# V' of all 128 tokens by whole-array products, its 32-token windows regrouped by DMA

## What is computed

```
qkv = x @ Wqkv;  q, k, v: 16 heads of 64
q = rotary(l2norm(q) * qs);  k = rotary(l2norm(k) * ks)
# windows of 32 queries against their own 32 keys and the 32 before
sim = q_window @ k_pair^T * 8, masked;  attn = softmax(sim)
out = attn @ v_pair
y = concat_heads(out) @ Wo + x
```

## Time and profile before

| | us |
|---|---|
| median of 3 runs | 3826.66 |
| lowest and highest run | 3822.85, 3828.74 |
| profiled execution, its own time | 3842.17 |
| span of its trace | 3840.4 |
| busy time of PE, DVE, ACT, POOL | 3503.5, 2839.2, 2381.7, 2295.0 |
| PE busy in the slots at 658.07 to 674.14 | 16.07 of 16.07 |

### The profile page before, as it was taken

One profiled execution on the slowest core, in us unless ns is written; L12 is line 12 of the kernel. 1 busy time (PEld: TensorE's weight loads), 2 busy tenths in 40 slices (PEclk: granted clock), 3 DMA queues, 4 the chain that ended last, 5 costly groups with the idle time before them and its releaser, 6 DMA issues.

```text
span 3840.4 us, 129350 instructions
## 1 busy us (share of the span) xinstructions
PE 3503.5 (91%) x51660; PEld 1890.2 (49%) x51660; DVE 2839.2 (74%) x6058; ACT 2381.7 (62%) x4153; POOL 2295.0 (60%) x2171
## 2 busy tenths in 40 slices
PE   3799999999999999999676899999999999999997
PEld 2355555545545545554343455555545545545553
DVE  1788878878878878886324888878878878878883
ACT  1566766766766766766202567667667666666674
POOL 0676766667667667664001766766667666666661
PEclk6899999999999999999667999999999999999998
DMA  5000000000000000000000000001001001001000
GB/s 179 10 14 22 22 15 22 22 15 22 22 15 23 20 15 23 22 10 19 35 0 3 10 13 23 22 15 32 13 14 34 11 14 34 11 14 34 13 5 12
DMA packets 50171, 83.78 MB, mean 22 GB/s; under 512 B 7168, under 2 KB 37120, under 8 KB 47232
## 3 DMA queue, kind: packets, MB, share of 16 engines
q1 hardware_dynamic: 49536, 75.05, 6.2%
HBM read 67.69 MB, written 7.34 MB: 20 GB/s over the span
## 4 chain that ended last, share of the span: by engine, by line
PE 81%; issue 10%; DVE 4%; ACT 3%; DMA 1%; POOL 1%; SPq 0%; DVEq 0%; ACTq 0%; POOLq 0%
PE VS L869 18%; PE QA L809 17%; PE TB L828 10%; PE TB L893 9%; PE VS L916 7%; PE TB L852 5%; PE FB L942 3%; PE FB L943 3%; PE FB L951 3%; PE VS L907 2%; ACT KT L448 1%; PE TB L836 1%; PE FB L927 1%; PE FB L932 1%; DMA KT<-in_w_out 1%
## 5 line engine op out<-in xcount | busy, mean ns | idle before, releaser
L330 POOL TENSOR_TENSOR QN<-T 128x512 f32<-128x512 f32 x768 | 979.3, 1275 | 715.8 <-DVE T L595 715.8
L337 POOL TENSOR_TENSOR QN<-QN,RR 128x512 f32<-128x512 f32 x768 | 801.7, 1044 | 308.6 <-DVE RR L616 308.6
L809 PE MATMUL QA<-WQ,Y 128*128 128x512 f32 x1536 | 810.0, 625 | 66.9 <-DVE Y L681 26.1
L869 PE MATMUL VS<-MW,Y 128*32 128x512 f32 x6144 | 738.7, 598 | 2.8 <-DVE Z L668 2.8
L434 ACT ACTIVATE SQ<-QA 128x512 f32<-128x512 f32 x768 | 458.7, 597 | 285.8 <-PE QA L809 252.9
L595 DVE TENSOR_TENSOR T<-QA,TAB 128x256 f32<-128x256 f32 x1536 | 571.0, 412 | 4.4 <-issue 4.4
L590 DVE TENSOR_TENSOR T<-QA,TAB 128x512 f32<-128x512 f32 x768 | 522.9, 681 | 48.8 <-issue 21.6
L622 DVE TENSOR_TENSOR Y<-TB,Y 64x128 f32<-64x128 f32 x384 | 111.0, 289 | 568.2 <-PE TB L836 565.5
L454 ACT ACTIVATE V<-VS 128x512 f32<-128x512 f32 x768 | 461.1, 600 | 90.0 <-PE VS L869 89.4
L603 DVE TENSOR_REDUCE SSQ<-SQ 128x8 f32<-128x512 f32 x768 | 486.7, 675 | 0.0
L893 PEld LDWEIGHTS TB<-CST,QN 128*128 128x128 f32 x3072 | 358.4, 142 | 238.3 <-issue 189.6
(11 more groups left out here) (154 smaller groups left out, 4316.7 us busy)
## 6 DMA issues: line engine op xcount, KB each, us to landing
TAB<-in_tables SPq DMA_DIRECT2D x192, 128.0 KB, 2.1
WQ<-in_w_qk SPq DMA_DIRECT2D x48, 256.0 KB, 3.2
MW<-m_dram SPq DMA_DIRECT2D x12, 1024.0 KB, 4.9
m_dram<-QN SPq DMA_DIRECT2D x6, 1024.0 KB, 4.9
W1R<-in_w SPq DMA_DIRECT2D x12, 341.0 KB, 3.4
KT<-in_w_vt SPq DMA_DIRECT2D x6, 512.0 KB, 5.8
KT<-in_w_out SPq DMA_DIRECT2D x6, 512.0 KB, 6.6
W<-in_w SPq DMA_DIRECT2D x12, 192.0 KB, 2.3
```

The source lines that it names most:

```text
L330: po.tensor_tensor(QN[:, n % 2, k, :], T1[:, k, :], T2[:, k, :], ALU.add).then_inc(s_add, 1)
L337: po.tensor_tensor(heads(QN[:, m % 2, k, :]), heads(QN[:, m % 2, k, :]), RR[:, m % 2, 8 * k:8 * k + 8].unsqueeze(2).to_broadcast([P, 8, DH ...
L809: mm(QA[:, k % 2, :], Y[:, j * P:(j + 1) * P], WQ[:, k, :], start=True, stop=True).then_inc(s_qk, 1)
L869: last = mm(VS[32 * q:32 * q + 32, w % 2, :], Y[:, a:a + WIN], MW[:, q, :], start=True, stop=True, tile_position=(0, 32 * q), skip_group_c ...
```

## The change

TensorE now forms V' of a whole tile for one head group at a time: all 128 tokens are the stationary operand, 128 x 128, and the product fills the whole array. Its result has tokens on partitions, which `attend` can't use. ScalarE copies it to a new buffer `VN`, and SP then issues five DMAs for each head group, from SBUF to SBUF, 32 partitions x 2 KB each: one for each of the four windows, and a fifth that puts the last window into a buffer of its own, `VP`, for the next tile. `attend` waits for the DMAs' semaphore instead of ScalarE's. V4 has two tiles instead of four. ScalarE's copy waits for the DMAs of two tiles ago instead of an `attend`.

```diff
+def by_pair(m, it):
+    v = 320 * (m // 2 + 1)
+    return v if it is None else it * (160 * TPL) + v
...
-        V4 = sb("V4", [P, 4, 4, 512])
+        VN = sb("VN", [P, 2, 4, 512])
+        V4 = sb("V4", [P, 2, 4, 512])
+        VP = sb("VP", [P, 2, 512])
...
+                def v_windows(q):
+                    m = n - 4
+                    sp.wait_ge(s_ve, by_tile(4, m, it, q + 1))
+                    src = VN[:, m % 2, q, :]
+                    dst = V4[32 * q:32 * q + 32, m % 2, :, :]
+                    for w in range(4):
+                        sp.dma_start(dst[:, w, :], src[32 * w:32 * w + 32, :]).then_inc(s_vd[m % 2], 16)
+                    sp.dma_start(VP[32 * q:32 * q + 32, m % 2, :], src[96:128, :]).then_inc(s_vd[m % 2], 16)
                 if live(c + 3, 0, it):
                     need(sp, s_t12, by_tile(4, n - 1, it, 4))
                     table(c + 3)
+                if live(c, 4, it) and (it is None or c % TPL != TPL - 1):
+                    for q in range(4):
+                        v_windows(q)
...
                     for k in range(4):
+                        v_windows(k)
                         sp.wait_ge(s_qk, by_tile(4, n, it, k + 1))
                         qk_weights(nxt, k)
...
-                    after(ac, s_o, 1, m - 3, 0, it, s)
-                    nc.scalar.activation(V4[:, m % 4, w, :], VS[:, w % 2, :], ACT.Copy).then_inc(s_ve, 1)
+                    need(ac, s_vd[m % 2], by_pair(m - 2, it))
+                    nc.scalar.activation(VN[:, m % 2, w, :], VS[:, w % 2, :], ACT.Copy).then_inc(s_ve, 1)
...
-                    after(pe, s_ve, 4, m, 3, it, s)
+                    pe.wait_ge(s_vd[m % 2], by_pair(m, it))
...
-                                v = V4[:, (m - 1) % 4, 3, hq * P:(hq + 1) * P]
+                                v = VP[:, 1 - m % 2, hq * P:(hq + 1) * P]
...
-                    a = j * P + w * WIN
-                    for q in range(4):
-                        last = mm(VS[32 * q:32 * q + 32, w % 2, :], Y[:, a:a + WIN], MW[:, q, :], start=True,
-                                  stop=True, tile_position=(0, 32 * q), skip_group_check=True)
-                    last.then_inc(s_vp, 1)
+                    mm(VS[:, w % 2, :], Y[:, j * P:(j + 1) * P], MW[:, w, :], start=True, stop=True).then_inc(s_vp, 1)
```

More of the change, by code:

```diff
@@ L142, in build_macaron @@
         s_mw, s_wf, s_w2, s_qr, s_ret_in = sem("s_mw"), sem("s_wf"), sem("s_w2"), sem("s_qr"), sem("s_ret_in")
+        s_vd = [sem("s_vd0"), sem("s_vd1")]
         s_tab = [sem(f"s_tab{k}") for k in range(4)]
@@ L308, in _ @@
             po.sem_inc(s_y, NG)
-            po.memset(V4[:, 3, :, :], 0.0).then_inc(s_cst, 1)
+            po.memset(VP[:, 1, :], 0.0).then_inc(s_cst, 1)
             po.memset(EPS[:, :], 1e-5).then_inc(s_cst, 1)
@@ L822, in attend @@
                             if not prev:
-                                v = V4[:, m % 4, w, hq * P:(hq + 1) * P]
+                                v = V4[:, m % 2, w, hq * P:(hq + 1) * P]
                             elif w:
-                                v = V4[:, m % 4, w - 1, hq * P:(hq + 1) * P]
+                                v = V4[:, m % 2, w - 1, hq * P:(hq + 1) * P]
                             else:
-                                v = V4[:, (m - 1) % 4, 3, hq * P:(hq + 1) * P]
+                                v = VP[:, 1 - m % 2, hq * P:(hq + 1) * P]
                             last = mm(TB[32 * w:32 * w + 32, 1, 0:P], PT[:, m % 2, b, 32 * w:32 * w + 32], v,
```

## The result

The changed kernel takes 4442.7 us (median of 4 runs, 4423.6 to 4445.5) against 3824.8 us for the kernel before beside it. The ratio is 1.1602, with a 95% interval of 1.1579 to 1.1626: 618 us slower, where 56 us faster was forecast. The profiled execution took 4423.6 us, with a span of 4421.7.

What follows compares the result with a forecast made beforehand. TensorE was taken to bound the kernel. A gain of 109 us against 34 (stack ends), 10 (clock), 3 (stack starts) and 6 (WQ slots) gave -56 us: 3827 to 3771, given as 3770 us, range 3740 to 3865.

Steps and rivals of the forecast that it cites:

- the price of an issue: SP's queue: 20 DMAs a slot follow one another at 0.473 us, with bounds of 0.38 and 0.64 us.
- cover: Time from first head group's copy to next slot's `attend`: 12.1, 11.5, 13.2, 13.0 us for slot types 0 to 3.
- The need: Time a slot's DMAs take before `attend`: wake 0.1, plus 19 x 0.473 for issues, plus 2.1 landing, 11.2 us.
- 10 us for the clock: TensorE at its lower clock after six long waits at the stacks' ends, 1.7 us each, 10 us in all.
- The gain on TensorE: `project_v` as whole-array products saves 0.60 us a slot in 182 slots, 109 us in all.
- joints: Where PE enters and leaves column strips around `project_v`; claimed savings 0.26 + 0.15 + 0.19 = 0.60 us a slot.
- rival 2: Joints' price is not the strips': only 0.26 us a slot saved, 3833 us, no change; chance 0.09.
- The landing: Last V' DMA before `attend` lands 2.1 us after its issue, taken from a TAB load.
- MW "just fits": `MW` load behind its slot's 20 issues goes out about 706.8, lands 4.9 us later at 711.7, in time for next slot.
- The traffic was charged at nothing: DMA engines: each new DMA takes 0.2 us on them, less than SP's spacing; no time was added for it.
- Rival 1: Transfers come too late, `attend` waits in the loop's slots; 4205 us at spacing 0.64; chance 0.26.
- Rival 3: SP's queue is faster than thought: spacing 0.38 us, need 9.4 us, 3744 us; chance 0.15.

Runs made afterwards that it cites:

- experiment 4: Kernel before plus 20 unread side DMAs a slot, five each of four kinds (SBUF or HBM source, different shapes); single execution, 3880.3 us.
- experiment 5: Kernel after with every V' DMA reading HBM (`m_dram`) instead of `VN`, so V' is not used; 3870.9 us, 1.0097.
- experiment 1: Kernel before with whole-array products in `project_v` and no DMAs, so V' has the wrong layout; 3717.2 us, 0.970.
- experiment 7: Kernel after with four extra 384-column products, results overwritten, ahead of `attend`'s wait to keep PE's clock up; 4413.8 us, 1.1543.
- experiment 9: Fastest whole-computation kernel with its 16 DMAs reading HBM: 3744.0 us; kernel before with 20 unread side DMAs of 16 KB: 3905.8 us.
- experiment 2: Kernel before plus 20 DMAs of 64 KB a slot from V4 into buffers nobody reads; `attend` does not wait for them; 3915.1 us, 1.0216.
- experiment 3: Kernel after with V' formed one slot earlier and four `VP` buffers; 3829.0 us, 0.9993.
- The fastest kernel with the whole computation: Kernel after with V' one slot earlier, `MW` load issued behind two head groups, four V4 tiles, no `VP`, 16 DMAs a slot; 3761.0 us, 0.9819.
- experiment 6: Kernel after with fewer DMAs a slot, part of V' missing: 16 (no `VP` copies) 3916.8 us, 1.0219; 8 (windows 0 and 1) 3731.5 us, 0.9751.

## Why the prediction was wrong, step by step

**Which step failed.** It is the price of an issue: "one DMA follows another at 0.473 us when SP never waits", taken from loads that read HBM. A DMA from SBUF to SBUF takes 0.59 us to issue and follows at 0.63. The prediction had this value as its upper bound, 0.64, with a time of 4205 us for it, and gave everything above 3865 a chance of 0.13. Experiments 4 and 5 show it, the first by the length of the issue, the second by the time: 572 of 618 us hang on the source. (Some 26 of these are busy time of `scores`, 318.9 against 293.1.) The prediction chose between 0.38 and 0.64 by "no plain issue of one DMA after another is slower than 0.473". But each of those plain issues had an HBM source, and that was the row's condition, not a property of the queue. No copy from SBUF to SBUF stood in that trace, and its stores from SBUF to HBM, at 0.34 us, would have pointed the wrong way. So the price could not be read from it; what could be known was that the row was of another kind, with a cover of 0.3 us to spare.

**The need was short by another microsecond.** With 0.635 the sum is 0.1 + 19 x 0.635 + 2.05 = 14.2 us; measured are 15.5 to 15.6. In the trace of after, over 560 to 1880 us of SP's timeline, 84 of 1,267 copies have an issue more than 0.1 us longer than 0.59, by 64 us in all: 1.0 us for each 20 issues. The chain's issue of 1.76 us is one. Some 0.2 us more lie between the landing and `attend`. The prediction's case of 0.64 had a need of 14.4 us and came to 4205; with 1.2 us more in each of 192 slots it comes to 4435, and 4443 was measured. That the two agree so well is luck in part. The mended sum lies 718 us above experiment 1, and nearly all of it is waiting; the trace has 504 us of waiting, and the rest is slower work on TensorE. What makes these issues long stays open. They show up for HBM sources too (up to 1.95 us in experiment 4).

**Where the time lies.** The span of after is 703.6 us longer than that of experiment 1. PE's idle time before `attend` grew from 5.5 to 509.7 us, which is 504. PE's busy time grew from 3371.7 to 3570.8, which is 199, for the same instructions. The two make 703. The 199 us have two causes. The group that reads `V` in `attend`, 386.4 us in experiment 1, is now this:

```profile
L851 PE MATMUL TB<-V,PT 128*32 128x128 f32 x10752 | 514.6, 338 | 0.0
```

That is 128 us more; the `p_transpose` and `project_v` groups behind it have 15 us more each. These 158 us are the lower clock behind the waits: in experiment 7, with the clock kept up, the three groups are back at 385.0, 242.5 and 724.4 us, as in experiment 1 (386.4, 244.3, 723.0). Another 26 us are `scores` (318.9 against 293.2), which the copies stretch, and 15 us are spread. The prediction charged 10 us for the clock, since it saw long waits at the stacks' ends alone, and nothing for `scores`. Experiment 7 doesn't say how much of the 158 us a steady clock would give back, since a shorter `attend` also shortens the ring and the filling held some of them up.

**The gain on TensorE was right.** -109 was forecast, and experiment 1 gave 3717.2 where 3717.7 (3826.66 - 109) follows from it. The joints' 0.60 us a slot hold and the other engines took next to nothing back; rival 2 is out. The Trainium skill, TensorEngine Tiling (Array Packing), section Key Properties, says that a change of tiling mode drains the engine. The joints of the earlier trace rows and experiment 1 agree with it, and they add the price: 0.60 us a slot for the joints of two groups.

**The landing was right.** 2.1 us were taken, 2.0 is the median of the 145 landings in the chain of after, from the start of the issue. The Trainium skill, DMA: Bandwidth & Descriptors, section Anatomy of one DMA, puts about 2.0 us on each DMA, nearly all of it the completion, and calls the making of descriptors small (for the software path). The landing agrees. The issue on SP's path, which that section does not describe, is not small here: 0.59 us from SBUF to SBUF, and 20 of them are what bounds this kernel. The Trainium skill, DMA: Bandwidth & Descriptors, section Bandwidth, advises to batch DMAs to 1 MiB or more. That pointed the right way, though by another mechanism than bandwidth: the DMA engines were 29.6% busy.

**MW "just fits" was wrong.** With issues at 0.63 and more the load goes out 14.3 us behind the first copy, not 9.6, and it lands in up to 6.1 us instead of 4.9. Why it lands later is open: a quarter of the bytes ahead of it changed nothing (experiment 9). Each time costs 5.6 us (experiment 2) to 6.4 us (experiment 3) on average, ten times. In the kernel after little of it shows (6.4 us of idle time in all, since `attend` waits anyway); in experiments 2 and 3 it stands free, and moving it gave 52 us back.

**The traffic was charged at nothing.** The fastest kernel with the whole computation is still 44 us over experiment 1, and experiment 2 had 27 us outside the `MW` slots. Of the 44, 22 us are `scores` (315.3 against 293.2), and a source in HBM gives 17 back. What remains, 27 us in 192 slots, is open.

**The rivals.** Rival 1 came true, by the mechanism and place that it names, with its upper bound of the spacing, and 238 us above the time that it gives for it. Experiment 5 at 0.46 us and experiment 6 at 16 DMAs lie near the knee, the kernel after far beyond it. Even at 0.46, though, the time was 3871 and not 3770. The covers of 11.5 us left no room for the long issues (0.7 us in a slot of that kernel) and for the landing of 2.8 us in place of 2.1, and the `MW` load came on top. So the forecast would have missed by 100 us with the right spacing as well, and would have had the wrong sign. Rival 3 is out.

## What to carry to other kernels

When a change puts many small DMAs on one queue ahead of a wait, price the queue first: number of issues times spacing, plus one landing, against the time from the first producer to the consumer. Take the spacing from issues with the same source and target, and if only another kind stands in the trace, let the upper bound decide when the margin is a few per cent. If it doesn't fit, start the work a slot earlier before giving the idea up (4443 to 3829 us here), and then look at what the new issues have pushed back in the same queue (3829 to 3777) and which of them can be left out (3777 to 3761).

## What was not expected of the hardware

- Back to back, SP's issue of a DMA takes 0.59 us from SBUF to SBUF and 0.42 us from HBM to SBUF. From SBUF to SBUF 16 or 64 KB and 32 or 128 partitions made no difference (experiment 4). Behind a pause the issues take 0.51 and 0.31 us, and from SBUF to HBM 0.34.
- Copies from SBUF to SBUF that are issued during a dense run of 128 small products on TensorE stretch it from 1.48 us to 1.61 to 1.68 us (median) and leave the length of a single product as it was; with 16 KB each nearly as much as with 64, with HBM as source not at all (experiments 2 and 9).
- In the kernel after, 225 of 3,840 V' copies (one in 17) have an issue more than 0.1 us longer than the others, by 0.7 us in the middle case and 1.9 at most; with HBM as source 174 of 3,840 (experiment 5). The cause is open.
- Behind its wait, `attend` ran in part of the slots of the kernel after at TensorE's lower clock: 3.64 us for the 64 matmuls, at a granted clock of 0.50, instead of 1.95. In the 53 slots with a wait of 0.3 to 2.0 us they took 1.95 or 1.96 in each; in the 57 with a wait of more than 3.5 us they took 3.2 to 3.64 us in 47 and 1.95 in 3. Between these lengths either happens.
